# A two-layer graph network on one core: edge keys made by ScalarE, window totals split in two, lookups reordered, three copies at the seam moved

## What is computed

```python
h = relu(layernorm(x)); agg = segment_sum(h[src], dst); t = relu(h + agg) through Linear(64,128), relu, Linear(128,128)
agg = segment_sum(relu(t)[src], dst);                   x = x + Linear(128,128), relu, Linear(128,64) of (relu(t) + agg)
h = relu(layernorm(x)); y = mlp3(h)                     # 64 -> 128 -> 128 -> 64
z = segment_sum(y[src], dst);                           x = x + mlp3(concat(h, z))
```

## Time and profile before

| | us |
|---|---|
| median of 3 runs | 923.52 (922.7 to 924.86) |
| the profiled execution's own time | 923.8 |
| its span, first to last instruction | 921.9 |
| PE busy / PEld busy | 862.5 (94%) / 710.6 (77%) |
| DVE / ACT / POOL busy | 697.5 (76%) / 479.4 (52%) / 395.4 (43%) |
| mean granted clock of PE | 0.987 |

### The profile page before, as it was taken

One profiled execution on the slowest core, in us unless ns is written; L12 is line 12 of the kernel. 1 busy time (PEld: TensorE's weight loads), 2 busy tenths in 40 slices (PEclk: granted clock), 3 DMA queues, 4 the chain that ended last, 5 costly groups with the idle time before them and its releaser, 6 DMA issues.

```text
span 921.9 us, 25227 instructions
## 1 busy us (share of the span) xinstructions
PE 862.5 (94%) x11291; PEld 710.6 (77%) x11291; DVE 697.5 (76%) x658; ACT 479.4 (52%) x573; POOL 395.4 (43%) x281
## 2 busy tenths in 40 slices
PE   0588999999899999899999999999999999999998
PEld 0367898999898999678877777777778866777776
DVE  7879999999999997385545656654565676787785
ACT  2753646655444454274545555454545555555543
POOL 5888888888000000307645566410110143444532
PEclk9989899999999999999999999999999999999999
DMA  3025255444443244405444344434433567888873
GB/s 112 19 88 156 85 156 157 132 139 130 143 143 122 95 143 143 136 23 160 119 140 121 104 129 127 127 99 134 121 99 86 150 196 204 229 237 244 230 218 107
DMA packets 81856, 126.85 MB, mean 138 GB/s; under 512 B 10160, under 2 KB 58544, under 8 KB 81616
## 3 DMA queue, kind: packets, MB, share of 16 engines
q1 hardware_dynamic: 78608, 121.98, 44.0%
q0 software_dynamic: 3136, 3.22, 1.7%
HBM read 84.22 MB, written 40.94 MB: 136 GB/s over the span
## 4 chain that ended last, share of the span: by engine, by line
PE 55%; ACT 1%; DVE 1%; issue 1%; POOL 0%; POOLq 0%; DVEq 0%; ACTq 0%
PE net_ps_hi L1343 15%; PE net_ps_lo L1343 15%; PE net_ps_lo L1360 7%; PE net_ps_hi L1360 7%; PE net_ps_mt L1288 5%; PE net_ps_ft L1288 2%; PE net_ps_check L1378 1%; PE net_ps_hi L1288 1%; PE net_ps_lo L1288 1%; ACT net_wide L1171 1%; PE net_ps_mt L1390 1%; DVE net_wide L867 1%; PE net_ps_mt L1430 0%; ACT net_hid L1174 0%; PE net_ps_ft L1297 0%
## 5 line engine op out<-in xcount | busy, mean ns | idle before, releaser
L1343 PE MATMUL net_ps_hi<-net_wide,net_first 128*128 128x512 f32 (+2 forms) x637 | 246.7, 390 | 0.0
L1343 PE MATMUL net_ps_lo<-net_wide,net_first 128*128 128x512 f32 (+2 forms) x637 | 238.8, 378 | 0.0
L867 DVE CAST net_wide<-net_raw 128x3584 fp32r<-128x3584 uint8 (+2 forms) x90 | 206.9, 2306 | 41.8 <-PE net_ps_lo L1360 15.8
L1171 ACT ACTIVATE net_wide<-net_raw 128x3584 fp32r<-128x3584 uint8 (+2 forms) x64 | 193.6, 3025 | 79.1 <-PE net_ps_lo L1343 46.3
L607 PE MATMUL build_ps_out<-build_parts_pad,build_cnts 128*128 128x195 bf16 x2401 | 226.7, 254 | 1.0 <-ACT build_cnts L474 1.0
L345 DVE TENSOR_TENSOR build_hot_lo<-build_grid_lo,build_keys_t 128x4096 bf16<-128x4096 bf16 x98 | 220.4, 2281 | 0.0
L607 PEld LDWEIGHTS build_ps_out<-build_parts_pad,build_cnts 128*128 128x128 fp8e4 x2401 | 206.8, 100 | 5.3 <-ACT build_cnts L474 1.1
L474 ACT ACTIVATE build_cnts<-build_ps_cnt 128x980 uint16<-128x980 f32 (+2 forms) x173 | 148.9, 912 | 117.8 <-PE build_ps_cnt L587 115.4
L1343 PEld LDWEIGHTS net_ps_hi<-net_wide,net_first 128*128 128x128 f32 x637 | 119.7, 188 | 28.0 <-issue 7.5
L1343 PEld LDWEIGHTS net_ps_lo<-net_wide,net_first 128*128 128x128 f32 x637 | 119.9, 188 | 23.0 <-issue 2.6
L867 POOL CAST net_wide<-net_raw 128x3584 fp32r<-128x3584 uint8 (+2 forms) x28 | 84.8, 3030 | 109.7 <-PE net_ps_hi L1360 53.1
(11 more groups left out here) (192 smaller groups left out, 712.1 us busy)
## 6 DMA issues: line engine op xcount, KB each, us to landing
net_raw<-edge_counts SPq DMA_DIRECT2D x154, 448.0 KB, 3.7
edge_counts<-build_cnts SPq DMA_DIRECT2D x168, 224.0 KB
net_raw<-edge_counts SPq DMA_DIRECT2D x14, 336.0 KB, 3.3
net_raw<-edge_counts SPq DMA_DIRECT2D x14, 224.0 KB, 2.6
xres<-in_x SPq DMA_DIRECT2D x1, 1568.0 KB, 7.1
out<-xres SPq DMA_DIRECT2D x11, 128.0 KB, 4.2
build_rows<-in_dst_rows,build_row_i POOLq DMA_INDIRECT x49, 3.9
build_edges<-in_edges,build_start_i POOLq DMA_INDIRECT x49, 3.4
```

The lines of the kernel that those rows point to most:

```text
L867: return issue(expanded[e % WIDE_RING][:, 0:n, :, :].rearrange("p w a d -> p (w a d)"), raw[e % RAW_RING][:, 0:n, :, :].rearrange("p w a d ...
L1171: expand(act, lambda to, x: nc.scalar.activation(to, x, ACT.Identity), e).then_inc(grown["act"], 1)
L1343: last = nc.tensor.matmul(ps[(b + 1) % 2][:, 0:n * P], first[:, c, lo:lo + H], expanded[e % WIDE_RING][:, 0:n, k, :], start=(c == 0), stop ...
```

## The change

1. **Keys.** `find_keys` leaves DVE. For each pair ACT now makes four bf16 rows straight from the bytes of `edges`: `take_bytes` (three instructions, L429 to L431 of the new text: low byte / 64, second byte x -4, sign of low byte - 127.5) behind piece 0 of the pair two before, and `take_distances` (two instructions, L438) behind piece 1. PE combines and turns them in four products instead of two transposes, into fp32 PSUM; ACT's copy multiplies by 64, and the ramps are scaled to match.
2. **Groups and lookups.** `SPANS` is 2 and then fours. Comparisons of a group stand 6 pairs and starts 5 pairs ahead of its first pair; POOL gathers the rows of group g+2 behind the edges of group g.
3. **Totals.** `total` adds up one window; the two of a pair stand behind the first and the third `lane_hots`.
4. **First pairs.** The keys of pairs 1 and 2 are turned and copied one by one; `use(0)` waits for the bf16 parts by sevenths.
5. **Seam.** For the last three blocks the copy of the high part goes from DVE's `split_y` to ACT (`upper_y`); the last block's `split_y` stands ahead of DVE's widening; ACT's `upper` of block 11 stands behind its widening.
6. **End.** SP reads the flag and branches ahead of its last two stores, which now stand in the branch's other arm.
7. The check on POOL works from `edges` (`tally_keys`: 5 instructions and the tree, before 6 and the tree); `edges` stays allocated in `net` in place of `keys`.

```diff
-SPANS = [(0, 2), (2, 6), (6, 10), (10, 14), (14, 18)] + [(w, min(w + 2 * STEP, NW)) for w in range(18, NW, 2 * STEP)]
+SPANS = [(0, 2)] + [(w, min(w + STEP, NW)) for w in range(2, NW, STEP)]
 def compare_step(g):
-    return {4: (1, 2), 5: (3, 0)}.get(g, (FIRST_PAIR[g] - 6 - 2 * (g - 6), 0))
+    return {4: (2, 1), 5: (4, 1)}.get(g, (FIRST_PAIR[g] - 6, 1))
 def starts_at(g):
-    return {3: (1, 1), 4: (2, 1), 5: (4, 1)}.get(g, (FIRST_PAIR[g] - 5 - 2 * (g - 6), 1))
+    return {3: (1, 3), 4: (3, 1), 5: (5, 1)}.get(g, (FIRST_PAIR[g] - 5, 1))
...
                 for g in range(2, len(SPANS)):
                     gather_edges(g, *SPANS[g])
-                    for later in ROWS_BEHIND.get(g, ()):
-                        gather_rows(later, *SPANS[later])
+                    if g + 2 < len(SPANS):
+                        gather_rows(g + 2, *SPANS[g + 2])
...
-                def total_pair(u):
+                def total(w):
-                        if q == 0 and u >= 3:
-                            total_pair(u - 3)
+                        if q in (0, 2) and u >= 3:
+                            total(2 * (u - 3) + q // 2)
...
+                def take_bytes(u):
+                    g = group_of(u)
+                    to = key_bytes[:, u % BYTE_RING, :, :].rearrange("p k (w e) -> p k w e", e=RUN)
+                    source = edges[:, 2 * u:2 * u + both(u), :, :].bitcast(U8).broadcast_to([P, 2, RUN, 4])
+                    act.wait_ge(edges_in[g], 16 * (SPANS[g][1] - SPANS[g][0]))
+                    nc.scalar.activation(to[:, 0, :, :], source[:, :, :, 0], ACT.Identity, scale=1 / 64)
+                    nc.scalar.activation(to[:, 1, :, :], source[:, :, :, 1], ACT.Identity, scale=-4.0)
+                    nc.scalar.activation(to[:, 2, :, :], source[:, :, :, 0], ACT.Sign, bias=cut[:, 0:1])
+                def take_distances(u):
+                    to = key_bytes[:, u % BYTE_RING, 3, :].rearrange("p (w e) -> p w e", e=RUN)
+                    for t in range(2):
+                        w = min(2 * u + t, NW - 1)
+                        last = nc.scalar.activation(to[:, t, :], edges[:, w, :, 1], ACT.Identity, bias=node128[:, w:w + 1],
+                                                    scale=float(-P))
+                    last.then_inc(keyed, 1)
...
                         copy_counts(u, k)
+                        if 0 < u < NU - 2 and k == 0:
+                            take_bytes(u + 2)
+                        if 0 < u < NU - 2 and k == 1:
+                            take_distances(u + 2)
...
                 def turn_keys(u, to):
-                    pe.wait_ge(keyed, group_of(u) + 1)
-                    for k in range(2):
-                        last = nc.tensor.transpose(to[:, k, :], keys[:, k, 2 * u:2 * u + 2, :].rearrange("p w e -> p (w e)"),
-                                                   ident_b[:, :])
+                    pe.wait_ge(keyed, u + 1)
+                    low, tile, top, away = (key_bytes[:, u % BYTE_RING, i, :] for i in range(4))
+                    nc.tensor.matmul(to, top, minus_b[:, None, :].broadcast_to([P, 2, P]), start=True, stop=False)
+                    nc.tensor.matmul(to[:, 0, :], low, ident_b[:, :], start=False, stop=False)
+                    nc.tensor.matmul(to[:, 1, :], tile, ident_b[:, :], start=False, stop=False)
+                    return nc.tensor.matmul(to[:, 1, :], away, ident_b[:, :], start=False, stop=True)
...
-                                pe.wait_ge(totalled, u - 1)
+                                pe.wait_ge(totalled, 2 * (u - 1))
...
                     dve.wait_ge(y_high, b + 1)
-                    v.tensor_copy(by_turn(second[:, w, 0:F], b), turned_view(high_f, b))
+                    if b < BLOCKS - 3:
+                        v.tensor_copy(by_turn(second[:, w, 0:F], b), turned_view(high_f, b))
...
-                flagged = flag(sp)
-                for b in range(BLOCKS - 4, BLOCKS):
+                for b in range(BLOCKS - 4, BLOCKS - 2):
                     store(sp, b)
```

181 lines of the change are left out of this document (96 added, 85 removed).

## The result

| | before | changed |
|---|---|---|
| median | 923.67 (922.7 to 924.9, 13 runs) | 918.92 (909.58 to 920.93, 13 runs) |
| ratio | | 0.994, 95% interval 0.9921 to 0.9959 |
| span of the profiled execution | 921.9 | 918.0 |
| mean granted clock of PE | 0.987 | 0.989 |

The forecast was 910.2, between 907 and 916. The direction was right, the size was not. The spread is itself a finding: before, 13 runs lie within 2.2 us; now twelve lie between 917.1 and 920.9 and one at 909.58. Where the runs of a kernel spread, as in the first four experiments, the ratios leave out those that lie over 1.5% above its fastest.

The account below looks back on a forecast made before the run. DVE was taken to bound `build` and PE `net`, with PE binding `build` after the change. -12.6 per pairs, +1.5 for first pairs and -2.2 at the seam sum to -13.3: 910.2 us, between 907 and 916.

Parts of the forecast that it names:

- What bound the kernel before: DVE sets the pace of `build`, PE that of `net`; key bursts on DVE and PE's waits lengthen the pairs.
- PE and DVE per pair: In `build`: PE 12.70 us per pair, DVE 12.79; PE binds without waits, -12.6 us over 21 pairs.
- The four products: PE's turn of keys in `build`: four products instead of two add 0.21 us per pair, between 0.09 and 0.32.
- the lead that I counted on: In `build`, DVE running ahead by one `hot_lo`, 2.23 us, would cover its being slower by 1.9 us over 21 pairs.
- my sign for PE's bound: In `build`, DVE would have idle time for the first time, with turns of keys 12.7 us apart.
- ACT's keys: ACT in `build`: five key instructions take 1.40 us per pair, with 0.4 us of slack, and cost nothing.
- First pairs: Start of `build`: first turn 0.6 us later, plus 0.9 for keys of pairs 1 and 2; +1.5 us together.
- Seam: Seam: two waits of PE lose 1.0 us each and the copy's move gives 0.2 more: -2.2 us.
- The rest: End of kernel, POOL's load, tail of `build` and middle of the passes: 0 us.
- Gathers: POOL's gathers in `build`, needed earlier and made in groups of four: cost nothing, hidden behind two pairs of other work.
- ACT waiting for edges: ACT in `build`: listed among the signs that the forecast is wrong; no size given.
- The range: Whole kernel: 907 to 916.0 us, with under 0.2 chance outside it.

Follow-up runs that it names:

- the first four experiments: Changed kernel with totals in one reduction, or two back to back; kernel before with split totals, or new seam: 948.36, 950.03, 936.44, 931.17 us, against 932.1 before.
- the second profiled run of the changed kernel: Changed kernel, unmodified, run again on a chip like the first: median 918.83 us (911.75 to 920.67); the profiled run was the lowest, 911.75.
- early starts: Changed kernel with comparisons of groups 9 to 12 and starts of groups 8 to 12 moved ahead: 910.30 us, 0.9858 of the kernel before.
- the totals together: Changed kernel with both 128x65 reductions of a pair back to back behind the first one-hot: 950.03 us, ratio 1.0212.
- the kernel before with the split: Kernel before with only the totals split, a 128x65 reduction behind the first and third one-hot: 936.44 us, ratio 1.0065.
- the version with one reduction per pair: Changed kernel with a pair's totals in one 128x130 reduction behind the first one-hot: 948.36 us, ratio 1.0185; 914.36 us on a chip like the first.

## Why the prediction was wrong, step by step

**What bound the kernel before**: right. DVE's bursts and the waits behind them are gone, and PE takes over.

**PE and DVE per pair**: right. Forecast 12.70 for PE; measured 12.65 to 12.66. The four products take a place of 0.37 (203.96 to 204.33) where two took 0.21: +0.16, forecast +0.21. For DVE I had 12.79, and where it sets the pace, in the second profiled run of the changed kernel, six pairs from 103.49 to 180.30 take 12.80 each. So the lead that I counted on does not cover DVE in every run, and my sign for PE's bound, idle time of DVE, did not come: with early starts DVE has none over 0.3 us from 71.3 to 348.5 while PE keeps to 12.66.

**ACT's keys**: the cost of nothing was right, the duration too high. In the changed kernel they stand so:

```profile
201.20 0.31 ACT L429 ACTIVATE build_key_bytes<-edges 128x128 bf16<-128x128 uint8 x1
201.40 0.31 ACT L430 ACTIVATE build_key_bytes<-edges 128x128 bf16<-128x128 uint8 x1
201.59 0.40 ACT L431 ACTIVATE build_key_bytes<-edges,build_cut 128x128 bf16<-128x128 uint8 x1
201.89 0.98 ACT L469 ACTIVATE build_cnts<-build_ps_cnt 128x980 uint16<-128x980 f32 x1
202.75 0.58 ACT L438 ACTIVATE build_key_bytes<-edges,build_node 128x64 bf16<-128x64 int16 x2
```

The three take 0.69 (201.20 to 201.89) and the two 0.48 (202.75 to the next start at 203.23), 1.17 in all; the forecast had 1.40 from the comparison's row. The Trainium skill (ScalarE: Activation LUTs, What ACT_TABLE_LOAD costs) gave an estimated 1.17, and the trace agrees. The first two, with no bias from SBUF, take a place of 0.20 each; reading every fourth byte costs nothing extra that shows.

**First pairs**: +1.5 was too much. The first turn came at 23.72, 0.06 later than before and not 0.6; ACT's key work takes 1.42 us from its start at 22.30 to the turn, DVE's took 1.23, and the edges were in 0.13 sooner; `use(0)` came at 55.58, 1.4 later, forecast 55.7. But the turn in pair 1 came at 66.61 against 63.55, and the next was level again, 77.00 against 76.91. The start costs 0.1 us where I had 1.5, for the delay is made good in the pair behind it.

**Seam**: right. -2.2 forecast; -2.0 alone on the kernel before, 2.3 in the windows. The waits of 1.49 and 1.76 are gone; of the same two one of 0.65 is left.

**The rest**: right. From PE's last instruction to the end of the span it is 3.4 us in both.

**Gathers**: this is the step that failed: "I cost this at nothing, hidden behind two pairs of other work. Without that cover DVE's and PE's stop would be the length of a gather." The first sentence is wrong, and the second named too short a stop: what it put at nothing is a stall of 9.9 us. I counted gathers at the pace of the kernel before, in which POOL always had a start in hand; the change asks for them later, so that POOL waits, and a POOL that has waited can come back into a mode in which it gets 2.3 gathers per pair instead of 5. It then runs short of the 4 that it needs, and after five pairs ACT stands 9.55 us. Of the signs in my list, "ACT waiting for edges" was the nearer one; it waited for rows. Without this step the sum comes out: with early starts the median is 13.3 us below the kernel before, as forecast (the profiled span, 907.3, is 14.6 below; the start's 1.4 is most of the difference); the stall gives back 9.9 in the profiled run of the changed kernel, and 17 of its 19 runs lie at 917 us or more. That it lands on the forecast to a tenth is in part luck, since the start was too dear by 1.4 and the runs of the version with early starts spread over 1.8.

**The range** left this case out because I gave the gathers no bound. The row of a gather held for 7.8 us was not in the trace of before, but the count was: 4 gathers per pair on an engine that from 100 to 200 us was busy for 87.18 of 100, beside a DVE that leaves no gap. A wait of POOL for starts, and a queue that has to catch up behind it, deserved a rival.

**A version that beats both** came out of the test: early starts, with one reduction per pair, 909.08 us, 14.5 below the kernel before. One reduction or two makes no difference that these runs can tell, once the mode is not entered.

## What to carry to other kernels

A helper engine with slack on paper may need its slack in one piece: look at what it waits for, and at the rate at which it can catch up, not at its busy share. When a lookup is made later, ask whether the engine that serves it will now stand still between requests; here the request made earlier was worth some 8 us (0.9858 of the kernel before instead of 0.9945). And when twelve runs lie at one time and one lies ten microseconds below, the low one can show what the edit does without an accident that the others share: it is worth a profile of its own.

## What the runs showed of the hardware that I had not expected

- POOL's indirect DMA, 0.95 us alone, waits for an edge between two large DVE instructions, and in one mode any edge will do (at most 3.4 us), in the other only one with a reduction or a start (4.4 and 7.8 us with two per pair, 12.4 with one). Entered only behind a wait of POOL: in 8 of the 34 waits of over 1 us for a start behind 78 us, in all traces together. Left when DVE stood still (for 6.1 us in the changed kernel, for 0.27 us with the totals together), and once, in the kernel before with the split, behind four short instructions of `find_keys` without a pause. What in the chip holds the state is open. In all 34 POOL comes back 0.34 to 0.36 us into the one-hot behind the start, and in the second profile of the changed kernel a wait of 4.18 us led to nothing and one of 4.19 into the narrow mode. So neither the length of the wait nor that instant tells the eight from the rest. Whether it is the wait or the instant that makes the entry possible no run separated.
- A DVE instruction of one column (0.08 us of its time) between two one-hots is enough: with it at each edge no gather from 80 us on takes over 3.2 us.
- On one of the chips PE's issue gaps between small products came to 16.0 us in the version with one reduction per pair, where the changed kernel had 0.7 on the first chip, and the kernel before took 8 us more there, with a spread of 19. Their cause was not looked for.
